# Experts from dense to sorted: tokens gathered by expert on chip, in a two-layer decoder

## The reference

```
s      = sigmoid(xn @ gate_w.T + lb_bias)       8 experts
top2   = the two best experts of each token
w      = s of the two, divided by their sum
share  = per expert: mean of w over the tokens that chose it (all 8192 are looked at)
expert = (silu(xn @ gate[x].T) * (xn @ up[x].T)) @ down[x].T     hidden size 128
out    = x + sum over the token's two experts of share[x] * expert_x(xn)
           + shared expert(xn), hidden size 256
```

## Time and profile before

| | |
|---|---|
| median of three timed runs | 3944.82 us (3943.13 to 3945.25) |
| profiled execution, its time | 3942.24 us |
| its span in the profile | 3940.5 us |
| TensorE busy | 3470.4 us, 88% |
| VectorE busy | 3004.2 us, 76% |
| ScalarE busy | 2335.2 us, 59% |
| GpSimd busy | 1292.5 us, 33% |

### The profile page before, as it was taken

The page is one execution under the profiler, slowest core; times in us unless marked ns, Lnnn a source line. Parts: engine busy times, 40 slices in busy tenths (PEclk is TensorE's granted clock), DMA queues, the critical chain, the costliest instruction groups (busy, mean ns, idle before and its releaser), DMA issues. The chain is left out here.

```text
span 3940.5 us, 99801 instructions
## 1 busy us (share of the span) xinstructions
PE 3470.4 (88%) x28590; PEld 2987.8 (76%) x28590; DVE 3004.2 (76%) x9366; ACT 2335.2 (59%) x8540; POOL 1292.5 (33%) x4876
## 2 busy tenths in 40 slices
PE   3779999999999999999968888888888699999999
PEld 2768788887878788878856777777777578888888
DVE  4368888898888889888836777777777666666666
ACT  1346767777676777677736777777777433333332
POOL 0024444343444444443413555555555300000000
PEclk8569999999999999999978999999999889999999
DMA  4001000000000000000010000000000010000000
GB/s 144 9 19 32 27 29 32 24 32 24 32 24 32 24 32 25 31 31 25 27 30 13 16 16 16 17 18 16 16 16 16 19 35 11 12 11 11 12 11 12
DMA packets 76031, 96.49 MB, mean 24 GB/s; under 512 B 12592, under 2 KB 65344, under 8 KB 75968
## 3 DMA queue, kind: packets, MB, share of 16 engines
q1 hardware_dynamic: 69696, 86.52, 6.9%
q0 software_dynamic: 2176, 8.39, 0.6%
q10 hardware_dynamic: 4096, 0.83, 0.1%
HBM read 78.67 MB, written 17.04 MB: 24 GB/s over the span
## 5 line engine op out<-in xcount | busy, mean ns | idle before, releaser
L365 POOL TENSOR_TENSOR tiny<-tiny 128x1 f32<-128x1 f32 x3456 | 775.4, 224 | 1524.2 <-DVE tiny L352 1281.5
L712 ACT ACTIVATE work<-bank,att 128x128 f32<-128x128 f32 x2048 | 720.9, 393 | 74.6 <-DVE att L702 74.6
L173 PE MATMUL bank<-w1r,workr 128*128 128x256 f32 (+2 forms) x1536 | 557.4, 363 | 13.1 <-DVE workr L1785 12.0
L175 PE MATMUL bank<-w1r,workr 128*128 128x256 f32 (+2 forms) x1536 | 513.7, 334 | 0.0
L174 PE MATMUL bank<-w1r,workr 128*128 128x256 f32 (+2 forms) x1536 | 513.5, 334 | 0.0
L712 ACT ACTIVATION_READ_ACCUMULATOR work<-bank,att 128x1 f32 x2048 | 477.9, 233 | 0.0
L731 PE MATMUL bank<-const,work 128*128 128x128 f32 x2048 | 326.2, 283 | 148.3 <-ACT work L712 113.6
L702 DVE TENSOR_REDUCE att<-bank 128x4 f32<-128x512 f32 x512 | 333.8, 683 | 152.8 <-PE bank L695 148.7
L193 PE MATMUL bank<-work,w0p 128*128 128x128 f32 x3072 | 432.9, 281 | 5.0 <-ACT r_tfi_ L1072 2.5
L2146 ACT ACTIVATE work<-bank 128x256 f32<-128x256 f32 x320 | 123.0, 384 | 489.0 <-PE bank L175 489.0
L193 PEld LDWEIGHTS bank<-work,w0p 128*128 128x128 f32 x3072 | 391.6, 195 | 20.3 <-ACT r_tfi_ L1072 3.4
(11 more groups left out here) (254 smaller groups left out, 8082.5 us busy)
## 6 DMA issues: line engine op xcount, KB each, us to landing
work<-decay_sums SPq DMA_DIRECT2D x64, 512.0 KB, 3.6
work<-in_ctx SPq DMA_DIRECT2D x128, 128.0 KB, 2.0
x_res<-in_x POOLq DMA_DIRECT2D x8, 1024.0 KB, 20.5
recurrence_out<-r_xo_ SPq DMA_DIRECT2D x64, 128.0 KB, 1.7
work<-recurrence_out SPq DMA_DIRECT2D x64, 128.0 KB, 2.1
out_dram<-work SPq DMA_DIRECT2D x64, 128.0 KB, 1.7
work<-in_L_attn_in_proj_w SPq DMA_DIRECT2D x10, 128.0 KB, 12.6
work<-in_L_ffn_expert_gate_w SPq DMA_DIRECT2D x8, 128.0 KB, 2.3
```

The lines of the kernel that those rows point to most:

```text
L173: pe.matmul(out_, lhs[0], rhs[0], start=first, stop=False)
L175: return pe.matmul(out_, lhs[1], rhs[0], start=False, stop=last)
L365: e.tensor_tensor(out_, a_, b_, ALU.add if b_ is three_halves else ALU.mult)\
L712: last = e.activation(Pb[g % 2][:, c * P:c * P + P], sc_banks[g % 2][:, c * P:c * P + P], ACT.Exp, bias=a_nm[:, 4 * g + c:4 * g + c + 1], ...
```

## The change

The routed experts are computed only for the tokens that chose them.

- In layer 1, ahead of its Newton steps, GpSimd clears a buffer, writes row numbers into it, and fills an array of 136 x 128 rows in HBM (`slots`, 258 numbers a row: the token's 256 and two index words) by four DMAs. The phase waits for them at its end.
- In `route` the choice mask is counted per tile and expert (eight one-column products), turned into each row's rank within its expert (three products on TensorE), and each expert gets whole slots of 128 rows: at most 136. `where` holds, for both choices of a token, the row in `slots` and the row in the result array; `owner` holds the expert of each slot; `share` the two factors of a token. The weights' 38 jobs are split into 12 and 26 around this.
- `experts` has three loops. The first goes over 64 tiles: the shared expert (one group in place of five), whose result is added to `x_res`; the normalised row with its index words is doubled (`twin`, on ScalarE) and GpSimd scatters both copies by indirect DMA, 128 rows each. The second goes over 136 slots: SP loads a slot, TensorE transposes it, reads the slot's expert into a register (`value_load`, once for `k_up` and once for `k_down`) and uses it in the weights' addresses; the hidden part has 128 columns; ScalarE copies the result out and GpSimd scatters it to the token's result row. The third goes over 64 tiles: SP fetches both result rows of each token, VectorE adds them with their factors, and ScalarE's queue stores the tile.
- `rounds` staggers the stages: `stage(back, do)` runs `do` for the item `back` before the current one, with rings of 4, 8 and 4 buffers.

The diff, cut to its core:

```
+TOKENS = 64 * P
+SLOTS = 2 * TOKENS // P + E
+R_UP, R_SLOT, R_TOK, R_END = C_END, C_END + P, C_END + P + SLOTS, C_END + P + SLOTS + 64
+ROW = D + 2
...
+        slots = nc.dram_tensor("expert_rows", (SLOTS * P, ROW), F32, kind="Internal").ap()
+        results = nc.dram_tensor("expert_results", (2 * TOKENS + 4 * P, D), F32, kind="Internal").ap()
+        wpos[0] = WORK - 4 * ROW
+        blank = wk(4 * ROW).rearrange("p (k d) -> p k d", k=4)
...
+                e.memset(blank, 0.0).then_inc(S["blank_ready"], 1)
+                e.wait_ge(S["blank_ready"], 1)
+                for k in range(4):
+                    e.iota(blank[:, k, D:D + 1].bitcast(I32), [[0, 1]], base=2 * TOKENS + k * P, channel_multiplier=1)\
+                        .then_inc(S["blank_ready"], 1)
+                e.wait_ge(S["blank_ready"], 5)
+                for k in range(4):
+                    e.dma_start(slots.rearrange("(s k p) d -> k p s d", k=4, p=P)[k],
+                                blank[:, k:k + 1, :].to_broadcast([P, SLOTS // 4, ROW])).then_inc(S["blank"], 16)
...
+        jobs2, jobs3 = jobs2 + jobs3[:6], jobs3[6:]
+        w2 = weights("w2", work[:, 0:4096], jobs2)
+        w3 = weights("w3", work[:, 0:4096], jobs3)
...
+                e.wait_ge(S["t_mask"], 1)
+                for x_ in range(E):
+                    last = e.matmul(bank[6][0:NB, x_:x_ + 1], t_mask[:, :, x_], const[:, C_ONE:C_ONE + 1], start=True, stop=True)
+                last.then_inc(S["t_tiles"], 1)
+                e.wait_ge(S["t_prefix"], 1)
+                e.matmul(bank[5][:, :], r_up, t_mask, start=True, stop=False)
+                e.matmul(bank[5][:, :], const[0:NB, C_ONE:C_ONE + P], t_pos[0:NB], start=False, stop=True)
+                e.matmul(bank[7][:, 0:E], const[0:NB, C_ONE:C_ONE + P], t_tiles[0:NB], start=True, stop=True)\
+                    .then_inc(S["t_rank"], 1)
+                e.wait_ge(S["w2_lo"], len(jobs2))
+                w3[1](e)
...
+                e.wait_ge(S["t_tiles"], 1)
+                link(e.tensor_scalar(t_tiles[0:NB], bank[6][0:NB, 0:E], 1.0, None, ALU.mult))
+                e.tensor_tensor(t_pos[0:NB], r_up[0:NB, 0:NB].unsqueeze(2).to_broadcast([NB, NB, E]),
+                                t_tiles[0:NB].unsqueeze(1).to_broadcast([NB, NB, E]), ALU.mult).then_inc(S["t_prefix"], 1)
+                e.wait_ge(S["t_rank"], 1)
+                link(e.tensor_scalar(t_whole, bank[7][:, 0:E], float(P - 1), None, ALU.add))
+                link(e.tensor_scalar(t_whole, t_whole, 7, None, ALU.arith_shift_right))
+                link(e.tensor_scalar(t_ends[0][:, 4:4 + E], t_whole, 1.0, None, ALU.mult))
+                for k, s_ in enumerate((1, 2, 4)):
+                    link(e.tensor_tensor(t_ends[k + 1][:, 4:4 + E], t_ends[k][:, 4:4 + E], t_ends[k][:, 4 - s_:4 - s_ + E], ALU.add))
+                link(e.tensor_tensor(t_start, t_ends[3][:, 4:4 + E], t_ends[0][:, 4:4 + E], ALU.subtract))
+                link(e.scalar_tensor_tensor(out=t_pos, in0=across(t_start), scalar=float(P), in1=by_tile(bank[5][:, :]),
+                                            op0=ALU.mult, op1=ALU.add))
+                for c, chosen in enumerate((t_first, t_second)):
+                    link(e.tensor_tensor(t_tmp, t_pos, chosen, ALU.mult))
+                    link(e.tensor_reduce(t_place[:, c, :], t_tmp, AX.X, ALU.add))
+                    link(e.tensor_scalar(where[:, :, c, 1], t_place[:, c, :], 1.0, None, ALU.mult))
+                later = t_later[0:1].rearrange("p (s e) -> p s e", e=E - 1)
+                link(e.tensor_tensor(later, r_slot[0:1].unsqueeze(2).to_broadcast([1, SLOTS, E - 1]),
+                                     t_ends[3][0:1, 4:4 + E - 1].unsqueeze(1).to_broadcast([1, SLOTS, E - 1]), ALU.is_ge))
+                link(e.tensor_reduce(t_count[0:1], later, AX.X, ALU.add))
+                link(e.tensor_scalar(owner, t_count[0:1], 1.0, None, ALU.mult))
...
-                e.tensor_tensor(coef, t_first, t_mean[:, 0:E].unsqueeze(1).to_broadcast([P, NB, E]), ALU.mult)\
...
+                for c, chosen in enumerate((t_first, t_second)):
+                    link(e.tensor_tensor(t_tmp, chosen, across(t_mean[:, 0:E]), ALU.mult))
+                    link(e.tensor_reduce(share[:, :, c], t_tmp, AX.X, ALU.add))
...
-        NG = 5
...
+        def rounds(e, n, ring, lag, step):
+            first = -(-(lag + ring) // ring) * ring
+            def one(h, k):
+                def stage(back, do):
+                    r = (k - back) % ring
+                    turn = h + (k - back - r) // ring
+                    i = ring * turn + r
+                    if not isinstance(h, int) or 0 <= i < n:
+                        do(i, r, turn)
+                step(stage)
+            for i in range(first):
...
+        RF, RK, RZ = 4, 8, 4
+        LF, LK, LZ = 5, 7, 3
...
+                for r in range(4):
+                    e.wait_ge(S[f"f_put{r}"], 32 * (NB // 4))
+                def load(i, r, turn):
+                    if used(i, 8):
+                        e.wait_ge(S["k_tr"], i - 7)
+                        e.sem_inc(S["sp_passed"], 1)
+                        e.wait_ge(S[f"k_put{r % 4}"], 16 * (2 * turn + r // 4 - 1))
+                        e.sem_inc(S["sp_passed"], 1)
+                    src = slots.rearrange("(s p) d -> s p d", p=P)
+                    src = src[i] if isinstance(i, int) else src[ds(i, 1)].rearrange("o p d -> p (o d)")
+                    e.dma_start(k_row[:, r, :], src).then_inc(S[f"k_row{r}"], 16)
+                rounds(e, SLOTS, RK, LK, lambda stage: stage(0, load))
+                for r in range(4):
+                    e.wait_ge(S[f"k_put{r}"], 16 * (SLOTS // 4))
+                def fetch(i, r, turn):
+                    if used(i, 4):
+                        e.wait_ge(S["z_o"], i - 3)
+                        e.sem_inc(S["sp_passed"], 1)
+                    src = results[0:2 * TOKENS, :].rearrange("(c b p) d -> b p c d", c=2, p=P)
+                    src = src[i] if isinstance(i, int) else src[ds(i, 1)].rearrange("o p c d -> p (o c) d")
+                    e.dma_start(z_row[:, r], src).then_inc(S[f"z_row{r}"], 16)
+                rounds(e, NB, RZ, LZ, lambda stage: stage(0, fetch))
...
+                def k_transpose(i, r, turn):
+                    q = r % 2
+                    e.wait_ge(S[f"k_row{r}"], 16 * (turn + 1))
+                    if used(i, 2): e.wait_ge(S["k_lo"], i - 1)
+                    for c in range(2):
+                        last = e.transpose(bank[6 + q][:, c * P:c * P + P], k_row[:, r, c * P:c * P + P], ident)
+                    last.then_inc(S["k_tr"], 1)
+                def k_up(i, r, turn):
+                    q = r % 2
+                    x_ = e.value_load(owner[0:1, i:i + 1] if isinstance(i, int) else owner[0:1, ds(i, 1)],
+                                      min_val=0, max_val=E - 1)
+                    e.wait_ge(S["k_lo"], i + 1)
+                    if used(i, 2): e.wait_ge(S["k_h"], i - 1)
+                    for k in range(2):
+                        last = mm3(e, bank[q][:, 0:2 * P], (f_T[q][:, 0, k, :], f_T[q][:, 1, k, :]),
+                                   (w_gu[:, 0, k, ds(x_ * (2 * P), 2 * P)], w_gu[:, 1, k, ds(x_ * (2 * P), 2 * P)]),
+                                   k == 0, k == 1)
+                    last.then_inc(S["k_gu"], 1)
+                def k_turned(i, r, turn):
+                    q = r % 2
+                    e.wait_ge(S["k_h"], i + 1)
+                    if used(i, 2): e.wait_ge(S["k_hlo"], i - 1)
+                    e.transpose(bank[2 + q][:, 0:P], f_h_[q][:, 0, :], ident).then_inc(S["k_htr"], 1)
+                def k_down(i, r, turn):
+                    q = r % 2
+                    x_ = e.value_load(owner[0:1, i:i + 1] if isinstance(i, int) else owner[0:1, ds(i, 1)],
+                                      min_val=0, max_val=E - 1)
+                    e.wait_ge(S["k_hlo"], i + 1)
+                    if used(i, 2): e.wait_ge(S["k_y"], i - 1)
+                    mm3(e, bank[4 + q][:, 0:D], (f_hT[q][:, 0, 0, :], f_hT[q][:, 1, 0, :]),
+                        (w_dn[:, 0, ds(x_, 1), :].rearrange("p o d -> p (o d)"),
+                         w_dn[:, 1, ds(x_, 1), :].rearrange("p o d -> p (o d)"))).then_inc(S["k_acc"], 1)
+                def slot(stage):
+                    stage(3, k_transpose)
+                    stage(4, k_up)
+                    stage(5, k_turned)
+                    stage(6, k_down)
+                rounds(e, SLOTS, RK, LK, slot)
...
+                def k_result(i, r, turn):
+                    q = r % 2
+                    e.wait_ge(S["k_acc"], i + 1)
+                    if used(i, 4): e.wait_ge(S[f"k_put{r % 4}"], 16 * (2 * turn + r // 4))
+                    e.activation(k_y_[:, r % 4, :], bank[4 + q][:, 0:D], ACT.Copy).then_inc(S["k_y"], 1)
...
+                def norm(i, r, turn):
+                    if used(i, 4):
+                        e.wait_ge(S[f"f_put{r}"], 32 * turn)
```

(34 more changed lines are left out.)

363 lines of the change are left out of this document (199 added, 164 removed).

## The result

| | before | after |
|---|---|---|
| median | 3943.98 us (4 runs) | 3986.29 us (4 runs, 3976.53 to 3989.17) |
| profiled execution | 3942.24 us | 3976.53 us |
| its span | 3940.5 us | 3974.8 us |

The ratio is 1.0103, 95% interval 1.0085 to 1.0122: slower by 1.0%, clear of the noise but under 2%. The forecast was 3878 us, faster; the time lies inside the range of 3755 to 3995.

A forecast was written before the change was run, and what follows sets the result against it. TensorE was taken to bound the experts' stretch. Experts 94.2 us less, with 16 (routing) and 12 (layer 1) back, gave 66.2 less: 3876.0 profiled, 3878 us as the median; range 3755 to 3995.

The forecast's parts named there:

- the start of layer 1: GpSimd's clearing, numbering and four filling DMAs delay the first tile by 12 us (0 to 45); the first loads hide.
- the experts: All three expert loops with fill and handovers: 673.4 us against 767.6, 94.2 less.
- routing: Routing block before the experts: added VectorE operations, products and handovers cost 16 us more, 12 to 22.
- The shared loop: First experts loop: two scatters of 1.45 us make GpSimd the slowest, 2.9 us a tile, 185.6 us for 64 tiles.
- The slots: Second experts loop, 136 slots: 2.7 us each, 367.2 us, of which 1.39 is TensorE's products and transposes.
- combining: Third experts loop: DMA packets set the pace, 1.5 us a tile, 96 us (83 to 122).
- the second handover: Between slots and combining: SP waits for every result before the first fetch, 8 us, 4 to 14.
- the clock: TensorE, though idle half of each slot, would not drop to half clock; a granted 0.5 would prove the forecast wrong.
- A: Rival in the slots: TensorE's queue hides the register loads, slot about 1.9 us, 109 us less, 3770; chance 0.22.
- B: Rival in the shared part: scatters occupy GpSimd longer; gain gone from 1.97 us each, 4000 us at 2.4; chance 0.16.
- C: Rival in the slots: loads and addresses cost double, or half clock; slot 3.4 us, 3974; gain gone from 3.19; chance 0.12.
- the rest: Remaining chance, 0.04: a start of layer 1 or a ring wait far worse than bounded.

The follow-up runs named there:

- fill_three: Changed kernel with the fourth filling DMA issued in GpSimd's pipeline step 9 of layer 1 instead of at the start: 3879.31 us.
- fill_spread: Changed kernel with the four filling DMAs issued one at a time in GpSimd's steps 6 to 9 of layer 1: 3882.49 us, ratio 0.9841.
- same_third: Changed kernel unedited, run a third time, in another chip session: 3918.05 us.
- load_of_two_b: fill_spread with one register load for two slots, its value copied at each use, no bounds tests: 3810.18 us, ratio 0.9672.
- one_load_b: fill_spread with one register load a slot instead of two, its value copied at each use, no bounds tests: 3820.05 us, ratio 0.9692.

## Why the prediction was wrong

Two steps failed, the start of layer 1 and the experts, and it took both to turn the sign: -66.2 + 43.4 is still -22.8; with the experts' 58.7 and routing's -1.6 it is +34.3.

**The start of layer 1** was forecast 12 us late, by 3.8 us of GpSimd for each filling DMA. Each takes 1.75 us to write, but the fourth is not taken until the first three are through, and the block is 58 us late at its first Newton step, 55.4 at routing. The other end that I gave, 45 us if GpSimd must wait until most rows have drained, named the mechanism and was too small: all 13.47 MB of the first three DMAs had moved before the fourth went in, 61 us after the first. That is 61 x 16 / 13,056 = 0.075 us a row on each engine, where I reckoned 0.062. I chose the value from a row of eight DMAs of 1024 rows, none of which made GpSimd stand, and had no row for DMAs of 4352. fill_three shows that three of them do not make it stand either; the fourth does, even with only the end of the third still to move (fill_spread). The same step held that the first tiles' loads hide; fill_spread shows 16.8 us of waiting for them.

**The shared loop** was forecast at 2.9 us a tile with GpSimd the slowest. The scatter was over-priced, 1.45 against 1.29, so two of them (2.58) lie just beside TensorE's 2.55, and the profiles of four of the six sessions, the first measurement counted as one, show 2.54. In same_third the stretch is 171.1 us, 31 less than forecast. In the first profile and in the third session it is 3.4 a tile and 226.5 us, from stands of ScalarE that the forecast did not know; they are worth 55.4 us, and without them the changed kernel is not slower: 3938.27 beside 3944.37, and 3918.05 beside 3935.47, one run each. The whole difference that was measured, 42 us, is thus smaller than this one effect, and so the sign hung on the session too, while the late start of layer 1 is in every unedited profile (first Newton step at 2120.2, 2130.8 and 2121.4 us).

**The slots** took 2.90 us, not 2.7 (32.5 us in all). The loads with their tests and addresses are worth 1.29 of it, forecast 1.30, though that value was the middle between two far bounds, and so partly luck; the part without them was under-priced, 1.61 against 1.39. The Trainium skill's floor of about 600 ns for a load (page "DMA: Bandwidth & Descriptors", "Latency and other measured facts") would give 2.8 with 1.61 for the rest, an estimate. The trace does not agree: a load took 0.30 us in `k_down`, 0.37 in `k_up`, and 0.54 where it filled two registers. What brings a place to 0.65 is what stands behind the load.

**Routing** (+14.4 against 16) and **combining** (1.54 us a tile against 1.5, DMA share 0.79) came as forecast, the second handover took 4.3 us against 8, and the clock came too: no half clock over the slots. In sum, same_third has its experts in 677.6 us against 673.4 forecast, but by errors that cancel: 31.1 less in the shared loop and 3.7 in the handover, 33.4 more in the slots and 5.6 in combining.

**The rivals.** A (loads hidden, a slot of 1.9) fell: 2.90. load_of_two_b has A's slot, 1.92, but with fewer loads and no tests; how much of its loads lies beside running products was not measured. B (a scatter over 1.97 us) fell: 0.98. C (a slot over 3.19) fell: 2.90. What came was in part the rest, at 0.04, a start of layer 1 worse than bounded; the stands of ScalarE were in no rival. The time lies in the range only because that reached to the times of B and C, and neither of their mechanisms came: that is luck.

## What to carry to other kernels

A DMA issued by GpSimd costs that engine its writing, and one that its queue does not take yet stops everything behind it there: put bulk fills where nothing waits behind them, and price the wait for those ahead to move, not only the writing. Where an engine's idle time is put down to issue, read the sequencer's own instructions by line: here they told that a register load was 0.30 us of the 0.90 to 1.14 us at its place, that two kernels had lost their loads, and that a load of two registers takes nearly twice as long as one. And where a difference of one per cent matters, look at the stages of a second session before explaining it: one program had two paces in one of its loops.

## What the runs showed of the hardware

- An indirect DMA that scatters 128 rows of 1024 or 1032 bytes costs GpSimd 0.98 us, with 0.30 between two; a plain one of 4352 rows 1.75 us. Three of these, 13,056 rows, are taken at once; the fourth right behind them stands for 56 to 65 us. It goes in within 1 us of the end of the third, also where the four were written some 18 us and more apart (fill_spread, 5.6 us of standing).
- On TensorE's sequencer a register load from SBUF took 0.30 us, one of two registers 0.54 (medians of one_load_b and load_of_two_b), a register step of an address 0.046.
- The same loop, instruction for instruction, runs at 2.54 or 3.4 us a tile, the same in all kernels of a session (four sessions of experiments with 2.54, one with 3.40 to 3.41, and the first profile with 3.44), while the kernel before differs by under 0.3%. The lost time is ScalarE standing, 56 times for over 1.0 us in 64 tiles, before its hardware loop as in it. What it stands for is open.
- TensorE idle for a third of the slots' stretch kept a granted clock of 0.99.
